# A graph block with linear attention: more one-hot marks made ahead of the waits, and x's high parts copied into the attention banks

## The reference, cut to what matters

```python
xn = layernorm(x)
# graph part: two layers, each h @ W.T + b, then a sum over edges into dst, then relu
h1 = relu(segment_sum((xn @ W1.T + b1)[src], dst)); gnn = relu(segment_sum((h1 @ W2.T + b2)[src], dst))
# mix part: linear attention, then two products and a residual
q = softmax(xn @ Wq.T, -1) * 512 ** -0.5
k = softmax(xn @ Wk.T, -2);  v = xn @ Wv.T
s = q @ (k.T @ v) + xn
mix = s @ mW1.T @ mW2.T + s
x = x + gnn + mix
# routed experts with Sinkhorn gates and top-k on layernorm(x), added to x
```

## Time and profile before

| what | value |
|---|---|
| median of three runs | 470.5 us (470.48 to 472.29) |
| the profiled execution, its own time | 470.02 us |
| its span (what the rows cover) | 468.1 us |
| PE busy | 449.9 us, 96% |
| DVE busy | 333.2 us, 71% |
| ACT busy | 150.3 us, 32% |
| POOL busy | 66.1 us, 14% |
| granted TensorE clock | full in all 40 slices |

### The profile page before, as it was taken

The page is one execution under the profiler, slowest core; times in us unless marked ns, Lnnn a source line. Parts: engine busy times, 40 slices in busy tenths (PEclk is TensorE's granted clock), DMA queues, the critical chain, the costliest instruction groups (busy, mean ns, idle before and its releaser), DMA issues.

```text
span 468.1 us, 7042 instructions
## 1 busy us (share of the span) xinstructions
PE 449.9 (96%) x2517; PEld 362.0 (77%) x2517; DVE 333.2 (71%) x1116; ACT 150.3 (32%) x274; POOL 66.1 (14%) x95
## 2 busy tenths in 40 slices
PE   8999999999999999899998999999999999888996
PEld 5877788889797979788787999877777775655783
DVE  5988599867868686888879960344545667777982
ACT  3666784223132323322240100223033124551120
POOL 5424700000000000000012000001400000006662
PEclk9999999999999999999999999999999999999999
DMA  8920200540000000203000000001844449405891
GB/s 250 265 78 2 90 0 1 137 97 11 1 1 0 2 1 8 85 0 127 1 5 2 2 0 1 1 0 20 296 131 133 133 135 366 170 1 169 295 366 73
DMA packets 20414, 40.46 MB, mean 86 GB/s; under 512 B 2521, under 2 KB 2851, under 8 KB 20373
## 3 DMA queue, kind: packets, MB, share of 16 engines
q1 hardware_dynamic: 18117, 32.53, 22.7%
q0 software_dynamic: 2256, 7.39, 4.5%
HBM read 30.09 MB, written 10.31 MB: 86 GB/s over the span
## 4 chain that ended last, share of the span: by engine, by line
PE 78%; DVE 13%; ACT 4%; issue 2%; DMA 1%; POOLq 0%; DVEq 0%; POOL 0%; SPq 0%
PE ps L769 29%; PE ps L1132 9%; PE ps L1024 9%; PE ps L952 6%; PE ps L897 6%; PE ps L756 4%; PE ps L970 2%; PE ps L811 2%; DVE RING_S L1877 2%; DVE RING_D L1876 2%; ACT scrap_a L1557 1%; DVE QTL L1811 1%; PE ps L1149 1%; ACT QTH L1287 1%; PE ps L945 1%
## 5 line engine op out<-in xcount | busy, mean ns | idle before, releaser
L1876 DVE TENSOR_SCALAR RING_D<-places,PLACES 125x170 bf16<-125x170 f16 x274 | 71.0, 259 | 3.2 <-issue 3.2
L1877 DVE TENSOR_SCALAR RING_S<-iota,HOME 125x128 bf16<-125x128 f16 x274 | 68.1, 249 | 0.0
L1024 PE MATMUL ps<-AT,H1H 125*128 125x416 f32 (+1 forms) x120 | 42.9, 358 | 0.3 <-ACT AT L1452 0.3
L1024 PE MATMUL ps<-AT,H1L 125*128 125x416 f32 (+1 forms) x120 | 42.2, 351 | 0.0
L756 PE MATMUL ps<-RING_D,RING_S 125*125 125x170 bf16 x274 | 35.2, 244 | 2.5 <-DVE RING_S L1877 0.9
L756 PEld LDWEIGHTS ps<-RING_D,RING_S 125*125 125x125 bf16 x274 | 27.5, 136 | 13.1 <-DVE RING_S L1877 7.1
L1132 PE MATMUL ps<-H2H,AT 125*125 125x512 f32 x90 | 36.1, 402 | 0.0
L1132 PE MATMUL ps<-H2L,AT 125*125 125x512 f32 x90 | 35.5, 394 | 0.0
L1149 PE MATMUL ps<-WE0H 128*128 128x512 f32 x129 | 35.5, 408 | 0.0
L630 POOL TENSOR_TENSOR G2L<-RAW_G,G2H 128x512 fp32r<-128x512 f32 x4 | 5.0, 1286 | 184.9 <-ACT G2H L1287 184.9
L1947 DVE TENSOR_TENSOR ps<-ps,bias 125x512 f32<-125x512 f32 x20 | 14.0, 699 | 20.4 <-PE ps L769 20.4
(11 more groups left out here) (413 smaller groups left out, 1156.5 us busy)
## 6 DMA issues: line engine op xcount, KB each, us to landing
RAW_E<-in_experts SPq DMA_DIRECT2D x8, 1024.0 KB, 9.9
RAW_AGAIN<-in_experts SPq DMA_DIRECT2D x3, 1024.0 KB, 9.5
X<-in_x SPq DMA_DIRECT2D x1, 2240.0 KB
out_x<-X SPq DMA_DIRECT2D x10, 224.0 KB
scratch<-X SPq DMA_DIRECT2D x10, 224.0 KB
scratch<-Y SPq DMA_DIRECT2D x10, 224.0 KB
RAW<-in_mW2T SPq DMA_DIRECT2D x4, 256.0 KB, 4.3
RAW_A<-in_mW SPq DMA_DIRECT2D x4, 256.0 KB, 4.7
```

The source lines that it names most:

```text
L1024: mm = pe.matmul(PS[plan[f"z{ch}_{f}"][0]][:, 0:c1 - c0], h[0:TT, k, 128 * f:128 * (f + 1)], AT[0:TT, k, c0:c1], start=(k == 0 and n == 0) ...
L1876: V.tensor_scalar(hot_d(v, width(b)), places[0:ET, 0:width(b)], PLACES[0:ET, c:c + 1], None, ALU.is_equal)
L1877: V.tensor_scalar(hot_s(v), iota[0:ET, :], HOME[0:ET, c:c + 1], None, ALU.is_equal).then_inc(done["marked"], 1)
```

## The change

- `visits_in_products`: each of the six spots in cp has 3 visits and not 2; a0 to a3 have 7 and not 8; x3, x5 and x7 have 7 and not 8; one visit more in h2. The ring of six slots so reaches to visit 23 (17 before).
- VectorE's list for the pairs is written anew, so that marks are made up to sixteen ahead, in front of the operations that wait for other engines.
- Five of the marks for z0_1 are made before VectorE reads the flag and branches, not after.
- `attend`: a half begins with one identity matmul of 504 columns for x's low part (for p = 0 two, low and high). For p > 0 the high part is put into the bank beforehand by a ScalarE copy (`put_x`), after the previous pair's low part is made (`sl_ready`), and TensorE waits for it (`xs_ready`).
- `turn_q(9)` moves from behind x7 into x7, in front of its matmul 7, into bank 6; ScalarE's `round_q(9)` moves ahead of the group stores of x7.
- POOL waits for all counts to be stored before it makes G2's low parts.
- The semaphores of two loads (wq, wv) are made one.

```diff
-                use(f"qt{i + 2}", (7,), ("qth_ready", i + 3), ("qtl_ready", i + 3))
+                use(f"qt{i + 2}", (7 if i + 2 < NT - 1 else 6,), ("qth_ready", i + 3), ("qtl_ready", i + 3))
...
-    spots = [("cp", n, 2) for n in range(12, 48, 6)]
+    spots = [("cp", n, 3) for n in range(12, 48, 6)]
...
-        spots += [(f"a{p}", 28, 8)]
+        spots += [(f"a{p}", 28, 7 if b < NT else 8)]
         if b < NT:
-            spots += [(f"q{b}", 6, 7), (f"x{a - 2}", 6, 7), (f"x{b - 2}", 6, 8)]
+            spots += [(f"q{b}", 6, 7), (f"x{a - 2}", 6, 7), (f"x{b - 2}", 6, 7 if p else 8)]
...
+            pool.wait_ge(done["adj_hi"], NG)
             for c in range(C):
                 split_lo("g2", c)
...
                     visits(f"a{p}", 28 * h)
+                    both = ps[:, 0:4 * (TT + 1)].rearrange("p (k t n) -> p k t n", k=2, t=2)
+                    if p:
+                        pe.wait_ge(done["xs_ready"], 2 * p + h - 1)
+                    for n, x in enumerate((XTL,) if p else (XTL, XTH)):
+                        pe.matmul(both, identr[:], x[:, 2 * p:2 * p + 2, 2 * h:2 * h + 2, 0:TT + 1].rearrange("p t k n -> p k t n"),
+                                  start=(p == 0 and n == 0), stop=False, skip_group_check=True)
                     for k in range(2):
...
-                        for n, x in enumerate((XTH, XTL)):
-                            pe.matmul(o, identr[:], x[:, 2 * p:2 * p + 2, f, 0:TT + 1], start=(n == 0), stop=False, skip_group_check=True)
...
                 for i in (2 * p, 2 * p + 1):
-                    mix(i)
-                    if i + 2 < NT:
-                        turn_q(i + 2)
+                    if i + 2 == NT - 1:
+                        mix(i, between=lambda: turn_q(NT - 1), at=7)
+                    else:
+                        mix(i)
+                        if i + 2 < NT:
+                            turn_q(i + 2)
...
+            def put_x(p, h):
+                act.wait_ge(done["sl_ready"], 2 * p + h - 1)
+                copy(ps_of(f"at{p}_{h}")[:, 0:4 * (TT + 1)].rearrange("p (k t n) -> p k t n", k=2, t=2),
+                     XTH[:, 2 * p:2 * p + 2, 2 * h:2 * h + 2, 0:TT + 1].rearrange("p t k n -> p k t n")).then_inc(done["xs_ready"], 1)
...
                 if b < NT:
                     scale_q(b)
+                    put_x(p + 1, 0)
+                    put_x(p + 1, 1)
                     round_q(a)
+                if b == NT - 1:
+                    round_q(b)
                 groups_ending(f"x{b - 2}")
-                if b < NT:
+                if b < NT - 1:
                     round_q(b)
```

and further down:

```diff
             h1_left(NT - 1)
+            mark_next(5)
             dve.wait_ge(loads["pairs"], 32)
...
-                    if u + 1 < 2 * C:
+                    if 0 < u < 2 * C - 1:
                         mark_next(5)
```

More of the change, by code:

```diff
@@ L431, in gps_block @@
         ld_w2 = [sem(f"ld_w2_{c}") for c in range(C)]
-        loads = {n: sem(f"ld_{n}") for n in ("edges", "wq", "wv", "b1", "b2", "g1",
+        loads = {n: sem(f"ld_{n}") for n in ("edges", "raw_a", "b1", "b2", "g1",
                                              "g2", "gate", "pairs", "x_again", *(f"again{g}" for g in range(1, 4)), *(f"exp{e}" for e in range(NE)))}
@@ L437, in gps_block @@
             "k_stored kmax_step diag_ready rmax_ready q_exp q_ready k_shift k_exp eh_ready el_ready "
-            "esum_step krs_ready e_used kmt_ready sh_ready sl_ready th_ready tl_ready cph_ready "
+            "esum_step krs_ready e_used kmt_ready xs_ready sh_ready sl_ready th_ready tl_ready cph_ready "
             "cpl_ready again_chain marked visited adj_hi q_inv qth_ready qtl_ready mix_added "
@@ L530, in load_weight @@
             def load_weight(name, w):
-                sp.dma_start(splits[name][0][:], rows(w)).then_inc(loads[name], 16)
+                sp.dma_start(splits[name][0][:], rows(w)).then_inc(loads["raw_a" if name in ("wq", "wv") else name], 16)
             load_pair(0)
@@ L953, in attend, with mix @@
                     closes(f"at{p}_{h}", mm)
-            def mix(i):
+            def mix(i, **kw):
                 p, t = i // 2, i % 2
                 product(f"xq{i}", opens(f"xq{i}")[0:TT, :], (lambda c: SH[:, c, t, 0:TT], lambda c: SL[:, c, t, 0:TT]), (rows_of(MPH), rows_of(MPL)),
-                        before=lambda c: pe.wait_ge(done["sl_ready"], 2 * p + c // 2 + 1), unit=f"x{i}")
+                        before=lambda c: pe.wait_ge(done["sl_ready"], 2 * p + c // 2 + 1), unit=f"x{i}", **kw)
             pe.wait_ge(*lo_of("wv", C - 1))
@@ L1295, in split_hi @@
                 else:
-                    act.wait_ge(loads[name], 16)
+                    act.wait_ge(loads["raw_a" if name in ("wq", "wv") else name], 32 if name == "wv" else 16)
                 copy(splits[name][1][:, c, :], splits[name][0][:, c, :]).then_inc(done["w_hi"], 1)
@@ L1909, in _ @@
                 a, b = 2 * p + 2, 2 * p + 3
-                mark_next(5)
+                mark_to(f"a{p}")
                 if a < NT:
                     q_peak(a)
+                    mark_next(3)
+                    q_inverse(a)
+                    mark_to(f"q{b}")
+                    attn_left(p, 0)
+                    mark_to(f"x{a - 2}")
+                    mark_next(2)
+                    attn_left(p, 1)
+                    mark_to(f"x{b - 2}")
+                    q_peak(b)
+                    mark_next(3)
+                    q_inverse(b)
+                    mark_to(f"q{a + 2}" if a + 2 < NT else f"a{p + 1}")
+                    add_mix(a - 2)
+                    q_left(a)
+                    if b < NT - 1:
+                        mark_next(3)
+                        add_mix(b - 2)
+                        q_left(b)
+                    else:
+                        q_left(b)
+                        mark_next(3)
+                        add_mix(b - 2)
                 else:
@@ L1915, in _ @@
                     split_lo("g1", 1)
[L1916 to L1923, removed]
+                    mark_to(f"x{a - 2}")
+                    attn_left(p, 0)
                     split_lo("g1", 2)
+                    attn_left(p, 1)
                     split_lo("g1", 3)
[L1926 to L1942, removed]
+                    mark_to(f"x{b - 2}")
+                    add_mix(a - 2)
+                    mark_to("h0")
+                    add_mix(b - 2)
             def add_bias(layer, i):
```

## The result

The changed kernel takes **456.13 us** (median of four runs, 456.0 to 456.58) beside 470.49 for the kernel before: a ratio of 0.969 (95% interval 0.966 to 0.971). The profiled execution took 456.16 us, span 454.3, 13.8 less than the 468.1 of before. Lines move by 1 to 22: the visits' matmul is L757, the marks L1893 and L1894, the matmul of mix and q L770, of attend L957, of z L1032.

The account below looks back on a forecast made before the run. TensorE, busy 96% of the span, was taken as the bound; 7.4 + 2.0 + 1.1 + 1.9 = 12.4 us off 470.02 gives 457.6, about 458.1 us as median, range 456.2 to 463.5.

Parts of the forecast that it names:

- the z0_1 term: Hole of 2.97 us at z0_1: POOL's move and five marks ahead of the branch give 2.0 us, bounds 1.0 and 2.7.
- the 0.5 us added for the median: Whole kernel: the median lies 0.5 us above the profiled execution, so 457.6 becomes about 458.1 us.
- the 0.4 us kept back on the marks: Pairs: held back from the marks' 7.9 us for places where they don't fit; the prediction says 0.5 us, its term 7.4.
- Marks in the pairs: Spots in x0 to x9 and q4 to q8: marks made ahead close TensorE's holes, 7.4 us, bounds 4 and 7.9.
- The layout of one pair: VectorE's new list laid beside TensorE for one pair: it fits at 83% busy, with one wait of some 0.2 us.
- turn_q(9): Before attend(4): turning inside x7 cuts TensorE's 1.30 us wait for QTL to 0.2, a gain of 1.1 us.
- Identity: Attend, pairs 1 to 4: one 504-column matmul replaces four of 252, 0.24 us saved in each of eight halves, 1.9 us.
- The copies: ScalarE's eight added copies, 0.65 us each, cost nothing; if their cover went, 1.3 us a pair, 5 us.
- late marks: Rival, pairs: half the marks still late, 4 of 7.4 us gained, 462 us; chance 0.19 shared with `put_x` waited for.
- marks that were no hole: Rival: the 32 waits lie over delays TensorE has anyway; only 4.0 us gained, 466.5 us; chance 0.06.
- the wait for `put_x`: Rival, attend: TensorE waits for `put_x` in each half, 5 us back, 463 us; chance 0.19 shared with half the marks late.
- the slower one: Rival, pairs: 21 marks ahead of operations TensorE waits for lose 4 us a pair, 16 us in four, 474 us; chance 0.04.

Follow-up runs that it names:

- old_branch: The changed kernel with the five marks of z0_1 put back behind the branch, POOL's wait kept: 457.58 us.
- put_x3: The changed kernel with each ScalarE copy of x into a bank made three times over, result the same: 459.40 us.
- old_list: The changed kernel with VectorE's former list for the pairs put back, all else kept: 464.49 us.
- put_x5: The changed kernel with each ScalarE copy of x into a bank made five times over, result the same: 475.59 us.
- nine_ahead: The changed kernel with all nine marks of z0_1 made ahead of the branch, not five: 456.18 us.
- old_pool: The changed kernel without POOL's wait, so G2's low parts are made beside the first z units: 460.03 us.
- before_third: The kernel before, unchanged, profiled once more to look for the fall of the granted clock: 472.42 or 472.37 us (the text does not say which).

## Why the prediction was wrong, point by point

The mechanisms were right; the sum was 2.0 us short. The step that failed most is the z0_1 term, mis-sized at 2.0 us where 2.6 to 2.7 were gained; next come the 0.5 us added for the median and the 0.4 us kept back on the marks.

- **z0_1: 2.0 forecast, 2.70 measured over the spot, 2.63 from h9.** "The rows favour neither end, so I take near the middle" was the failing step. Both halves were larger: 1.26 us for POOL (1.0 taken, the one held instruction of before) and 1.38 for the marks (1.0 taken). The sequencer ran ahead of all ten mark instructions, the good end; of their 1.7 us 0.34 went because the branch lands 4.18 us after the read where it was 3.84. And POOL held one instruction more than I counted, whose row stood in the trace of before, just ahead of the held RING_S: 0.49 us for 0.26, with the next started 0.42 us after it where 0.17 is usual, another 0.25 us beside the 1.06 of RING_S. Of these 1.31 us 0.06 went, since in `old_branch` the branch lands 3.90 us after the read (232.02 to 235.92) and not 3.84. The hole itself was read a little small, 2.97 us over a base of 0.91: z0_0's nine visits take 0.81.

```profile
246.92 0.49 DVE L1876 TENSOR_SCALAR RING_D<-places,PLACES 125x170 bf16<-125x170 f16 x1 [3.24 <-issue]
```

 The Trainium skill's queue of eight (Advanced Engine Details and Errata, Engine Queue Depths) gave 2.4 us; the trace has ten instructions still to start when the flag is read, two more than the rule has, and the measurement decides.
- **Marks in the pairs: 7.4 forecast, 7.8 measured.** All twelve spots closed. The 0.5 us kept back "for places where it doesn't" fit was not needed: VectorE at 84% (17.87 of 21.2) was late nowhere. The layout of one pair, with a least room of 1 us, had said so already.
- **turn_q(9): 1.1 forecast, 1.0 measured** (the 0.2 left is 0.15); and it depends on the list, since with the old one QTL is as late as before.
- **Identity: 1.9 forecast, 2.1 measured.** One matmul of 504 columns starts 0.23 us before the next. **The spots: 0 and 0.** **The copies: 0 and 0**, at 0.5 us each for 0.65 taken, with 1.8 us of cover for the 1 to 3 forecast; the price given for lost cover, 1.3 us a pair, fits what `put_x3` shows (each us past the cover is a us of wait).
- **The median above the profile: +0.5 us forecast, 0.0 measured.** The 0.5 was carried over from before to after as if it belonged to measuring. The kernel before spreads over 3 us from execution to execution, by the clock and by the cast at 4.3 us, and after's four runs lie within 0.6. Which of these made the 0.5 is not shown, since no clocks are on record for the four executions behind the 470.49. The spread of the cast may well be left in after: one execution of `old_list` took 466.55 us at a mean clock of 1.00, where the other three took 464.4 to 464.5.

By the parts: 7.8 + 2.6 + 1.0 + 2.1 = 13.5 us, with 13.8 measured in the spans; 0.3 us is not placed. The forecast's 12.4 lacks 0.4, 0.6 and 0.2, has 0.1 too much, and then 0.5 us were added for the median. The range's low end, 456.2, lay 0.5 us under the sum of the good ends of the terms, 456.7, as if they would not come together; they nearly did (13.5 of 13.8 us), and without the 0.5 us for the median the same good ends give 456.2. By how little the time missed the range, 0.07 us, is chance: the four executions lie from 456.0 to 456.58.

Of the rivals, late marks and marks that were no hole are refuted by the distances over the spots; the wait for `put_x` has no row; and the slower one, marks in front of what TensorE waits for, did not come, though `put_x5` shows that its kind exists: a delay in front of the turn counts from 1.8 us a pair on, and 5.0 us a pair (ten copies hold ScalarE for 6.04) make the kernel 0.9% slower than before (475.59 us, ratio 1.009, 1.007 to 1.011).

## What to carry to other kernels

Put filler work for another engine in front of an operation that waits, not behind it, and judge a late spot from the starts of the two products around it; where its end hangs on another engine, measure from a fixed point further ahead. Two moves that meet in one hole have to be priced together: the marks ahead of the branch are worth under 0.4 us while POOL's subtractions run, and 1.4 once these are gone. Where the executions of a kernel spread, ask which hole makes them spread before the offset between profile and median is carried to the next kernel.

## What the runs showed of the hardware

- A GpSimd subtraction of 128x512 fp32 (1.29 us) holds one VectorE instruction to its end: a mark 1.31 us for 0.26, the cast W1H 1.53 for 0.43.
- VectorE's sequencer reads a flag with ten instructions still to start; in `nine_ahead`, with eighteen of them, the read comes at 233.86 us, when ten are left again. From the read to the first instruction behind the branch it is 4.18 us in after (232.00 to 236.18) and 3.84 in before (243.08 to 246.92).
- In one profiled run (`old_pool`) the granted clock fell to 1.2 GHz behind a spot of 3.9 us in which TensorE did nine short visits, for 3.4 us, at a cost of 1.6; in six other profiled runs with a spot of 3.9 to 4.2 us it did not fall there. In nine executions with a spot of 2.5 to 2.6 us the mean clock is .997 or more. In `put_x5` it fell behind two of four stand-stills of 3.1 to 3.3 us.
- Where the first weight product starts at 5.93 us and not at 4.77 (`before_third`), the full clock is on record from 9.98 us on and not from 4.21, and TensorE loses another 1.1 us by its pace (0.43 us a matmul for 0.23).
- A ScalarE copy from SBUF into PSUM, 128x504 fp32, starts the next 0.5 us later.
